# Order of the low-rank weighting, the low-rank take and B in an adapted residual kernel in two layers

## The reference

```python
def _L0_cond_ref(x, conditions, weights):
    w = weights[conditions]
    return jnp.einsum('bct,bcd->bdt', x, w)

def _L1_cond_ref(x, W, A, Bm, scalings, adapter_idx):
    H = jnp.einsum('btd,od->bto', x, W)
    A_b = A[adapter_idx]
    B_b = Bm[adapter_idx]
    s_b = scalings[adapter_idx]
    xa = jnp.einsum('btd,brd->btr', x, A_b)
    delta = jnp.einsum('btr,bor->bto', xa, B_b)
    return H + delta * s_b[:, None, None]

x = x + _L0_cond_ref(x, itok_B_1_198, L0_cond_weights)
x = x + _L1_cond_ref(x, L1_cond_W, L1_cond_A, L1_cond_Bm, L1_cond_scalings, itok_B_0_6)
```

## Time and profile before

| what | value |
|---|---|
| median of 3 runs | 78.05 us |
| lowest, highest | 77.72, 78.56 us |
| span of the profiled execution | 76.0 us |
| its own time beside the span | not given by the page |
| PE busy | 71.5 us, 94% |
| PEld busy | 65.1 us, 86% |
| DVE busy | 55.2 us, 73% |
| ACT busy | 51.4 us, 68% |
| POOL busy | 33.6 us, 44% |
| granted TensorE clock | 1.000 |

### The profile page before, as it was taken

One profiled execution on the slowest core, in us unless ns is written; L12 is line 12 of the kernel. 1 busy time (PEld: TensorE's weight loads), 2 busy tenths in 40 slices (PEclk: granted clock), 3 DMA queues, 4 the chain that ended last, 5 costly groups with the idle time before them and its releaser, 6 DMA issues.

```text
span 76.0 us, 1936 instructions
## 1 busy us (share of the span) xinstructions
PE 71.5 (94%) x464; PEld 65.1 (86%) x464; DVE 55.2 (73%) x144; ACT 51.4 (68%) x126; POOL 33.6 (44%) x76
## 2 busy tenths in 40 slices
PE   3989999999999999999999999999999999999940
PEld 3957887785999699999999999999999999999930
DVE  4007954987979797979597968977797949675920
ACT  0725956995896597686768666968687767567440
POOL 5700591499799906354354515580655260000000
PEclk9999999999999999999999999999999999999999
DMA  0899479436789989578967963579416430303025
GB/s 0 208 417 390 118 213 236 142 113 205 234 284 281 306 276 294 210 243 225 302 207 214 311 220 70 151 201 312 156 39 237 138 138 4 138 13 138 0 97 179
DMA packets 9677, 14.55 MB, mean 191 GB/s; under 512 B 3650, under 2 KB 4418, under 8 KB 9666
## 3 DMA queue, kind: packets, MB, share of 16 engines
q1 hardware_dynamic: 7554, 9.16, 36.9%
q0 software_dynamic: 1536, 4.20, 18.4%
q10 hardware_dynamic: 576, 1.07, 4.5%
HBM read 10.23 MB, written 4.19 MB: 190 GB/s over the span
## 4 chain that ended last, share of the span: by engine, by line
PE 71%; DMA 9%; DVE 5%; issue 5%; ACT 4%; POOL 1%; POOLq 0%; ACTq 0%
PE z_ps L653 45%; PE z_ps L641 9%; DMA head<-head_a 5%; DMA b_raw<-b_t 4%; PE out_ps L708 4%; PE out_ps L709 3%; PE out_ps L695 3%; PE out_ps L713 3%; PE v_ps L687 2%; DVE b_stack L521 2%; DVE a_table L590 1%; ACT out_sb L413 1%; ACT a_table L427 1%; ACT x_high L387 1%; POOL b_raw L287 1%
## 5 line engine op out<-in xcount | busy, mean ns | idle before, releaser
L653 PE MATMUL z_ps<-moving,x_high 128*128 128x272 f32 x224 | 33.5, 290 | 0.0
L653 PEld LDWEIGHTS z_ps<-moving,x_high 128*128 128x128 f32 x224 | 29.9, 188 | 0.6
L287 POOL DMA_DIRECT2D b_raw<-b_t x32 | 16.1, 506 | 11.3 <-issue 5.2
L653 PE MATMUL z_ps<-moving,x_low 128*128 128x272 f32 x112 | 18.6, 288 | 0.0
L280 POOL CAST moving<-a_table 128x128 fp32r x28 | 9.1, 355 | 17.0 <-PE z_ps L653 14.3
L653 PEld LDWEIGHTS z_ps<-moving,x_low 128*128 128x128 f32 x112 | 15.8, 188 | 0.0
L512 DVE TENSOR_TENSOR z_low<-z_ps,z_high 128x272 fp32r<-128x272 f32 (+1 forms) x28 | 11.8, 422 | 1.4 <-ACT z_high L364 0.5
L521 DVE TENSOR_TENSOR b_stack<-b_raw,b_high 128x512 fp32r<-128x512 f32 x16 | 11.9, 741 | 0.2 <-ACT b_high L380 0.2
L380 ACT ACTIVATE b_high<-b_raw,group_sb 128x512 fp32r<-128x512 f32 x16 | 11.5, 716 | 0.2 <-DMA b_raw<-b_t 0.2
L364 ACT ACTIVATE z_high<-z_ps 128x272 fp32r<-128x272 f32 (+1 forms) x28 | 10.5, 376 | 0.2
L394 ACT ACTIVATE v_high<-v_ps,group_sb 128x128 fp32r<-128x128 f32 x16 | 5.8, 366 | 7.0 <-PE v_ps L687 6.9
(11 more groups left out here) (59 smaller groups left out, 76.6 us busy)
## 6 DMA issues: line engine op xcount, KB each, us to landing
b_raw<-b_t POOLq DMA_DIRECT2D x32, 128.0 KB, 3.2
out<-out_sb SPq DMA_DIRECT2D x15, 256.0 KB, 3.0
x_raw<-xt SPq DMA_DIRECT2D x13, 256.0 KB, 3.8
w_sb<-w SPq DMA_DIRECT2D x32, 16.0 KB, 3.1
w_late<-w_late_t SPq DMA_DIRECT2D x1, 480.0 KB, 6.9
head<-head_c ACTq DMA_DIRECT2D x1, 400.0 KB, 4.7
head<-head_d SPq DMA_DIRECT2D x1, 384.0 KB, 5.7
head<-head_a ACTq DMA_DIRECT2D x1, 264.0 KB, 3.5
```

The lines of the kernel that those rows point to most:

```text
L287: pool.dma_start(b_raw[s * C:(s + 1) * C, t % BBUFS, :], b_t[ds(which[s], 1), :, :].rearrange("a r (g n) -> (a r) g n", g=1) .to_broadcast ...
L653: last = nc.tensor.matmul(z_bank(t, part), x[:, t % XBUFS, k * P:(k + 1) * P], moving[:, int(n == HL), k, at:at + HALF], start=((n, k) == ...
```

## The change

It moves calls and adds or removes none.

- ACT, loop: `high_of_b(t)` goes from behind Z's A part to ahead of X and the low rank.
- DVE, prologue: `take_low_rank(1)` goes ahead of the low part of tile 2's W part; `low_of_w0` of tile 2's batch goes behind `low_of_v(1)` and `take_low_rank(2)`.
- DVE, loop: `low_of_b(t)` goes between the take and the low part of the low rank.
- PE: the weighting of tile 2 goes behind `a_bank(3)`; in the loop the weighting of t goes behind the last four of t's W bank. The last tile's order stays.

```diff
@@ scalar
             for t in range(3, last):
                 if t > 3:
                     high_of_z(t - 1, W_PART)
+                high_of_b(t)
                 if t + 2 < TILES:
                     high_of_x(t + 2)
                 high_of_low_rank(t)
                 high_of_z(t, A_PART)
-                high_of_b(t)
                 high_of_v(t)
                 take_out(t - 1)
@@ vector
             low_of_v(0)
             low_of_b(0)
+            take_low_rank(1)
             low_of_z(2, W_PART)
-            take_low_rank(1)
             low_of_b(1)
             low_of_x(3)
-            low_of_w0(BATCH_OF[2])
             low_of_v(1)
             take_low_rank(2)
+            low_of_w0(BATCH_OF[2])
             low_of_low_rank(2)
             low_of_z(2, A_PART)
             low_of_x(4)
@@
                 if t > 3:
                     low_of_z(t - 1, W_PART)
                 take_low_rank(t)
+                low_of_b(t)
                 low_of_low_rank(t)
                 low_of_z(t, A_PART)
                 if t + 2 < TILES:
                     low_of_x(t + 2)
-                low_of_b(t)
                 low_of_v(t)
@@ tensor
             a_bank(2)
             plain_layer0(1)
-            weigh_low_rank(2)
             last = TILES - 1
             for t in range(3, last):
                 a_bank(t)
+                if t == 3:
+                    weigh_low_rank(2)
                 w_bank(t, 0, 2 * K)
                 whole_layer0(t - 1)
+                w_bank(t, 2 * K, 3 * K)
                 weigh_low_rank(t)
-                w_bank(t, 2 * K, 3 * K)
             a_bank(last)
```

## The result

The changed kernel is slower: median 78.83 us (78.41 to 79.37, 4 runs) against 78.26 us for the kernel before in the same comparison (77.72 to 78.56, 4 runs), ratio 1.017 with a 95% interval of 1.011 to 1.023. That is 1.3 us. The ratio compares the fast executions alone, while the two medians, over all executions, lie only 0.57 us apart. The forecast was 0.55 us, 0.7%: right in sign, under half in size. 78.83 lies inside the range of 77.5 to 79.2.

The account below looks back on a forecast made before the run. PE, busy 94% of the span, bounds the kernel; only 0.67 us of gaps before 27 us can be won. Lost 0.58 plus 0.59, net 0.50, plus 0.05 at the last tile: 78.05 becomes 78.6 us, range 77.5 to 79.2.

Parts of the forecast that it names:

- PE has nothing to win beyond 27 us, 0.67 us in all before it: PE's timeline: full from about 27 us; before it, gaps of 0.26 and 0.41 us are all the change can win.
- constant of 2.05 us: Profiled span 76.0 us against median 78.05: the difference was treated as constant, and changes were added to 78.05.
- DVE's prologue is worth 0: Start, DVE: taking low ranks 1 and 2 earlier gains 0 us, with 0.05 lost at most.
- Tile 2: weighting at 20.04, a stall of 0.58 on B 2: PE at tile 2: weighting 1.23 us later, then L695 waits for B 2; 0.58 us lost, between 0.48 and 0.75.
- Tile 3: a stall of 0.59 at the weighting: PE at tile 3: reaches the weighting at 23.16, low rank 3's parts ready at 23.65; 0.59 us lost.
- so no wait: ACT at tile 3: B 3's rows land at 21.2, before ACT reaches B 3 at 21.72, so 0 wait.
- the middle for DVE's B 3: DVE at tile 3: free at 23.38, between 23.07 for a clean B 3 and 23.61 for one stretched beside POOL.
- Rival (c): Tile 3's weighting: late B 3 rows or full collision with L296, stall 0.82 to 1.1, time 79.0 us; chance 0.15.
- Steady loop, cost 0: Loop, weighting 0.50 us later: parts ready at 3.73, PE asks at 3.93, period stays 4.04; cost 0.
- rival (d): Loop: low rank late behind B and X on ACT, each of some twelve periods pays 0.1 or more, 79.8 us; chance 0.08.
- my bound of 1.2: Loop: most it could cost if the margin were gone, one exposed load of 0.1 us per tile, 1.2 in all.
- The Trainium skill's rule on the shared port: DVE's B 3 beside POOL: whoever starts first excludes the other; DVE free near 23.27, sum 0.11 us lower; left unsettled.

Follow-up runs that it names:

- e1: The kernel before, unchanged, run again against itself: ratio 0.998 (0.992 to 1.004).
- e7: The kernel before with only the two reorderings of DVE's prologue: ratio 0.999 (0.994 to 1.004).
- e2: The changed kernel, unaltered, run again against the kernel before: ratio 1.015 (1.010 to 1.021).
- e5: The kernel before with only PE's weighting of tile 2 moved behind A bank 3: ratio 1.008 (1.005 to 1.012).
- e12: The changed kernel with only DVE's move of B undone, ACT's kept: ratio 1.015 (1.006 to 1.025).
- e14: The changed kernel with PE's old order from tile 5 on: ratio 1.015 (1.008 to 1.022) against the kernel before.
- e10: The changed kernel with POOL loading B of tiles 2 and 3 ahead of its wait for the A table: ratio 1.008 against the kernel before.
- e3: The changed kernel without the moves of B on ACT and DVE: ratio 1.005 (0.999 to 1.011) against the kernel before.
- e4 to e7: Four parts, each alone in the kernel before: B's moves 1.002, PE's tile 2 1.008, PE's loop order 1.007, DVE's prologue 0.999.
- e4: The kernel before with only the moves of B on ACT and DVE: ratio 1.002 (0.994 to 1.010).
- e8: The kernel before with DVE's new prologue, tile 2's weighting inside A bank 3, tiles 3 and 4 weighted behind their W bank: ratio 0.992 (0.987 to 0.997).
- e9: The kernel before with the weighting inside A bank 3, tiles 3 and 4 weighted late, DVE's new prologue, and early loads of B: ratio 0.991.

## Why the prediction was right in sign and under half in size

- *PE has nothing to win beyond 27 us, 0.67 us in all before it*: the gaps of 0.26 and 0.41 were gone, as said. But the 0.67 was one execution's; e1 shows the kernel before with 0.6 us more at the start. Nor was the constant of 2.05 us between span and time one: the profiled executions of the changed kernel and of e1 have 1.64 (78.54 and 76.9) and 1.67 (78.07 and 76.4). So the profile before, whose own time is not on record, was probably of an execution faster than the median. The differences added to 78.05 are not touched by this.
- *DVE's prologue is worth 0*: 0.999 in e7.
- *Tile 2: weighting at 20.04, a stall of 0.58 on B 2*: weighting to 0.01 us; the stall was 0.69, and 0.66 in e2 and e5. Right, with e5 as its test.
- *Tile 3: a stall of 0.59 at the weighting*. **This is the term that was mis-sized: it measured 1.18 us**, above the 0.82 that the longest row had given. Two numbers in it failed. I let B 3's rows land as in the profile before, 2.8 us after issue, and wrote "so no wait"; in the changed kernel it was 3.8, and ACT waited 0.3, 0.8, 1.0 and 0.8 us in four profiles (profile after, e2, e12, e14). And I took the middle for DVE's B 3 because L296 starts late; POOL's casts of A, which my sum had left out, were enough to stretch it to 1.21. Rival (c) named the late rows and a full collision, though with L296. It should have been in the forecast: the wait costs at once while an early landing gains nothing, and the profile before itself had B's landings spread far wider than the one pair I took:

```profile
DMA to landing us min/median/max: 2.4/3.2/5.3
```

  e10 tests that term: without wait and collision the gap is 0.19. e3 and e5 show a third part that the forecast had at nothing: even without B in front of it, the low part of rank 3 itself collided with POOL (1.05 and 1.15 us instead of 0.22), and the gap was 0.51 and 1.10.
- *Steady loop, cost 0*. **This step failed too**: 0.32 us. I looked for a wait, and there is none; the margin that rival (d) doubted held (rank parts ready, ACT idle 1 us per tile). PE itself runs slower in the new order, 0.03 us per tile over ten or eleven tiles. I had no term for that, and my bound of 1.2 covered it for another reason.
- The Trainium skill's rule on the shared port (SBUF — State Buffer, "Who interferes with whom") has a VectorE operation with two SBUF inputs and a GpSimd one exclude each other for a whole instruction. I wrote that the trace doesn't settle it. Read by their ends, the rows of before bear it out:

```profile
22.34 1.15 DVE L489 TENSOR_TENSOR x_low<-x_raw,x_high 128x512 fp32r<-128x512 f32 x1
22.39 0.54 POOL L280 CAST moving<-a_table 128x128 fp32r x2
```

  The casts end at 22.93, X's low part at 23.49, L296 at 24.07, B 3 at 24.63: each some 0.56 us behind the one before it, as if in turns. In the profile after, the casts taken singly show turns again:

```profile
22.48 0.31 POOL L280 CAST moving<-a_table 128x128 fp32r x1
...
22.71 0.82 POOL L280 CAST moving<-a_table 128x128 fp32r x1
```

  The first cast ended at 22.79, unstretched; B 3 ended 0.60 behind it, at 23.39, and the second cast 0.15 behind that. What doesn't fit is who goes first. By the start of its record B 3 was 0.30 ahead of the first cast, and my reading of the rule would have had it done by 22.9. Why it still went second is not shown.

By terms from the profile: lost 0.69 + 1.18 + 0.32 = 2.19, won 0.67, net 1.5 us or 1.9%; the timed runs say 1.5 to 1.7%. The difference is smaller than the kernel before's own changing start (0.62 us between its two profiles). The parts one by one (e4 to e7) add to 0.2 + 0.8 + 0.7 - 0.1 = 1.6%. That is no proof of the sum: their intervals together are wider than 1%, and e4 and e5 each contain a gap at weighting 3.

## What to carry to other kernels

Moving a matmul later in a saturated engine's list closes the gap in front of it, but everything its result feeds moves by the same distance: count the chain from the new place to its next user, and move it by the least that closes the gap (four matmuls in e8, 0.992; twelve in e5, 1.008). The pair is not a clean test of that distance, since e8 also relieves tiles 3 and 4 and has DVE's new prologue; what is clean is the stall on B 2, 0.66 us in e5 and none in e8. An operation that waits for a transfer doesn't belong in front of the critical one in the same queue because the slot looked idle: it brings the transfer's whole spread with it. And look at the same stretch in several executions before pricing a wait by one.

## What was not expected of the hardware

- The same 29 matmuls per tile, back to back, take 4.02 and 4.06 us in turn in one order and 4.07 in another; the fast pace sets in two tiles after the order changes back (e9, e14), and e4, in the old order throughout, takes 4.07 twice behind the start before it falls to 4.02. Nothing waits in any of them. What in PE sets it is open; no run here was aimed inside it.
- A small VectorE operation with two SBUF inputs, 0.22 us, took 0.72 beside POOL's L296 in e1, 1.15 in e5 and, in e3, 1.05:

```profile
21.59 0.54 POOL L280 CAST moving<-a_table 128x128 fp32r x2
...
21.85 1.05 DVE L546 TENSOR_TENSOR low_rank_parts<-own_low_rank,low_rank_parts 128x32 fp32r<-128x32 f32 x1 [0.38 <-ACT low_rank_parts L409]
...
22.08 0.74 POOL L296 TENSOR_TENSOR w_sb<-w_sb,ident 128x256 f32<-128x256 f32 x1
```

It ended at 22.90, just behind POOL's L296 at 22.82; in e5 it ended at 23.31 behind 23.22, in e1 at 22.97 behind 22.87. In e3 and e5 it had begun beside a cast, and POOL's next instruction still came first. That is no rule: in e4 the same operation began at 22.36, inside the casts (22.15 to 22.75), and took its 0.22. A short operation on the critical chain can so cost as much as the long one beside it.
